# Edge groups' values by DMA copies, two images projected later, first maxima from two queues

## What is computed

```python
y = _layernorm(x)                         # then padded to 28 x 28, cut into 14 x 14 windows
qkv = win.reshape(Nw, 196, C) @ qkv_w + qkv_b
q, k, v = ...                             # 12 heads of 16 channels
attn = q @ k^T * scale + bias_h(q) + bias_w(q)   # relative positions, products of q
attn = softmax(attn)
o = attn @ v
x = shortcut + o @ proj_w + proj_b
x = x + fc2(gelu(fc1(_layernorm(x))))
```

## Time and profile before

| | us |
|---|---|
| median of 3 runs | 362.44 |
| the runs | 361.16 to 362.70 |
| the profiled execution, its own time | 361.79 |
| its span, first to last instruction | 359.7 |
| TensorE matmul busy in it | 340.2 (95%) |
| VectorE, ScalarE, GpSimd busy | 199.9, 146.9, 100.6 |
| mean granted TensorE clock | 0.995 |

### The profile page before, as it was taken

How to read it: one execution, slowest core, us unless ns; L and a number is a source line. 1 busy time by engine, 2 the same in 40 slices (tenths; PEclk the granted TensorE clock), 3 DMA queues, 4 the chain that set the end, 5 groups by cost and what they waited for, 6 DMA issues and landing times.

```text
span 359.7 us, 10564 instructions
## 1 busy us (share of the span) xinstructions
PE 340.2 (95%) x4494; PEld 259.9 (72%) x4494; DVE 199.9 (56%) x483; ACT 146.9 (41%) x326; POOL 100.6 (28%) x192
## 2 busy tenths in 40 slices
PE   6899899999988999999989979999998899999996
PEld 3467587889866548977837768878886643999576
DVE  6362668777767600126846466877785750145472
ACT  2188045555545442023119705555545452202330
POOL 3100507985312039200010050898431204000000
PEclk9899999999999999999999999999999999999999
DMA  7971000000012003010021000000000000000002
GB/s 212 386 244 40 3 5 4 3 6 4 3 24 99 22 1 111 0 66 2 0 89 25 9 3 3 5 3 4 5 5 4 0 2 0 0 2 0 2 0 89
DMA packets 9056, 13.34 MB, mean 37 GB/s; under 512 B 3153, under 2 KB 6609, under 8 KB 9010
## 3 DMA queue, kind: packets, MB, share of 16 engines
q1 hardware_dynamic: 9010, 12.67, 10.9%
HBM read 11.24 MB, written 0.79 MB: 33 GB/s over the span
## 4 chain that ended last, share of the span: by engine, by line
PE 88%; DVE 8%; issue 1%; SPq 1%; DMA 1%; ACT 0%; DVEq 0%
PE banks L912 17%; PE banks L884 13%; PE banks L1001 9%; PE banks L1019 9%; PE banks L929 8%; PE banks L843 6%; PE banks L800 4%; PE banks L771 2%; PE banks L760 2%; PE banks L1185 2%; PE banks L1032 2%; PE banks L1079 2%; DVE negmax L1427 2%; PE banks L819 2%; PE banks L1049 1%
## 5 line engine op out<-in xcount | busy, mean ns | idle before, releaser
L1264 ACT ACTIVATE arena<-banks 128x392 f32<-128x392 f32 (+2 forms) x144 | 62.5, 486 | 60.9 <-PE banks L912 60.9
L884 PE MATMUL banks<-attention_arena 32*128 32x196 f32 x384 | 49.1, 353 | 3.1 <-DVE negmax L1427 1.6
L912 PE MATMUL banks<-attention_arena 32*128 32x196 f32 x384 | 47.5, 342 | 3.3 <-ACT arena L1264 2.0
L1430 DVE TENSOR_REDUCE negmax<-banks 128x4 f32<-128x784 f32 x40 | 39.0, 974 | 14.6 <-PE banks L884 14.3
L912 PE MATMUL banks<-attention_arena,keys 32*128 32x196 f32 x384 | 44.3, 323 | 0.0
L884 PE MATMUL banks<-keys,attention_arena 32*128 32x196 f32 x384 | 44.1, 323 | 0.0
L912 PEld LDWEIGHTS banks<-attention_arena 32*128 32x128 f32 x384 | 30.1, 183 | 10.3 <-issue 7.2
L1001 PE MATMUL banks<-yT,fc 128*128 128x512 f32 (+1 forms) x96 | 33.3, 607 | 0.3
L1019 PEld LDWEIGHTS banks<-fc,arena 128*128 128x128 f32 x192 | 31.1, 190 | 1.5 <-ACT arena L1278 1.5
L884 PEld LDWEIGHTS banks<-attention_arena 32*128 32x128 f32 x384 | 28.2, 183 | 5.6 <-DVE negmax L1427 3.3
L912 PEld LDWEIGHTS banks<-attention_arena,keys 32*128 32x128 f32 x384 | 32.1, 184 | 0.0
(11 more groups left out here) (170 smaller groups left out, 641.2 us busy)
## 6 DMA issues: line engine op xcount, KB each, us to landing
fc<-in_fc SPq DMA_DIRECT2D x2, 768.0 KB, 5.5
qkv<-in_qkv SPq DMA_DIRECT2D x2, 576.0 KB, 4.1
fc<-in_fc SPq DMA_DIRECT2D x2, 576.0 KB, 5.5
attention_arena<-negmaxT SPq DMA_DIRECT2D x72, 1.0 KB
rel<-in_rel SPq DMA_DIRECT2D x2, 448.0 KB, 4.7
x_tok<-in_x SPq DMA_DIRECT2D x4, 192.0 KB, 3.1
inverse<-in_inverse SPq DMA_DIRECT2D x1, 768.0 KB
edge_rel<-negmaxT SPq DMA_DIRECT2D x48, 0.5 KB
```

What stands on the lines that cost most here:

```text
L884: ins = mm(o, asking, asked, start=not with_rel, stop=bool(with_rel))
L912: last = mm(m.bank[4 + j][:, cols * tile:cols * (tile + 1)], keys_of(slot, b, j, tile)[with_rel], queries_of(slot, b, j)[with_rel], start= ...
L1264: run(m.probsT[:, n % P_RING, j, 0:cols], m.bank[4 + j][:, 0:cols], ACT.Exp).then_inc(s.probs, 1)
L1430: dve.tensor_reduce(at[:, 4 * part:4 * part + 4].rearrange("k (j a) -> k j a", a=2), m.banks[:, 2 * part:2 * part + 2, 0:2 * MAIN_KEYS].re ...
```

## The change

Four things are done in each of the two attention blocks.

1. The "v_edge" jobs go, with GpSimd's gather `m.yEdge`. The edge groups' values are copied by SP's DMAs out of the images' rows of `m.v`: 5 DMAs per image (four of 6 or 8 single rows, one of 32 rows; a row is 432 floats, 1,728 bytes). Those of images 0 and 1 stand behind the key moves, as soon as ScalarE has taken the image's values out. Those of images 2 and 3 are issued one at a time behind the maxima of groups 1 to 10. `weigh` of an edge group waits for all 20. GpSimd clears, once at the start, the columns that the whole rows bring along.
2. `project` runs the short products of chunks 0 and 1 of the first half right behind `turn_norm` of the second half, ahead of the second half's full products.
3. The values of images 2 and 3 are projected behind the last rel_h job, ahead of `score` 0. They use banks 4 and 5, so `score` 1 waits until ScalarE has taken them out.
4. Group 0's four maxima DMAs are split: two from SP, two from ScalarE's queue.

```diff
+PROJ += [("v", n, 0, "act") for n in range(2)]
 PROJ += [("rel_w", n, 0, "act") ...] + [("rel_h", n, 0, "dve") ...]
+PROJ += [("v", n, 0, "act") for n in range(2, IMAGES)]
...
+            def move_edge_rows(s, b, piece):
+                if piece == 4:
+                    low = EDGE * SIDE
+                    to, of = m.v[low * b:low * (b + 1), TILES + 1], m.v[128 - low:128, 2 * b + 1]
+                else:
+                    tile, col = divmod(piece, EDGE)
+                    rows, at = min(WIN - 8 * tile, 8), EDGE * (WIN * b + 8 * tile) + col
+                    to = m.v[at:at + EDGE * (rows - 1) + 1:EDGE, TILES]
+                    of = m.v[WIN + col:WIN + col + SIDE * (rows - 1) + 1:SIDE, 2 * b + tile]
+                sp.dma_start(to, of).then_inc(s.v_moved, 16)
...
+                for b in range(2):
+                    wait_for(sp, s.proj_in, *taken_out(job("v", b, 0)))
+                    for piece in range(5):
+                        move_edge_rows(s, b, piece)
                 sp.wait_ge(s.edge_inputs, R_EDGES)
                 for n, (slot, b) in enumerate(GROUPS):
                     sp.wait_ge(s.maxT, n + 1)
+                    for block in range(2 if n == 0 else 0, 4):
+                        sp.dma_start(*max_rows_of(n, block)).then_inc(s.max_rows[n % M_RING], 16)
+                    if 1 <= n <= 10:
+                        move_edge_rows(s, 2 + (n - 1) // 5, (n - 1) % 5)
...
-                for short in (False, True):
-                    for j in range(first, last):
+                for short, jobs in ((False, range(CHUNKS)), (True, range(2)), (False, range(CHUNKS, 2 * CHUNKS)), (True, range(2, 2 * CHUNKS))):
+                    if short and 0 in jobs:
+                        turn_norm(s.ln[0], 0, 1)
+                    for j in jobs:
...
-                    elif h >= 2:
+                    elif h == 1:
+                        wait_for(pe, s.proj_in, *taken_out(job("v", IMAGES - 1, 0)))
+                    else:
                         pe.wait_ge(s.max, h - 1)
...
+                if b >= IMAGES:
+                    pe.wait_ge(s.v_moved, 16 * EDGE_ROWS)     # in weigh; EDGE_ROWS = 5 * IMAGES
...
-                project(l, 0, 2 * CHUNKS)
-                project_values(l)
-                project(l, job("v_edge", 0, 0), job("v_edge", 1, 0) + 1)
-                for j in range(job("rel_w", 0, 0), len(PROJ)):
+                project(l)
+                project_values(l, 0)
+                for j in range(job("rel_w", 0, 0), job("rel_h", SIDE // 2 - 1, 0) + 1):
                     relate(l, j)
+                project_values(l, 2)
...
+                act.wait_ge(s.maxT, 1)
+                act.wait_ge(s.edge_inputs, R_EDGES)
+                for block in range(2):
+                    act.dma_start(*max_rows_of(0, block)).then_inc(s.max_rows[0], 16)
```

More of the change, by code:

```diff
@@ L559, in split, with max_rows_of @@
             return ap[..., FULL * b:FULL * (b + 1)], ap[..., LEFT_AT + LEFT * b:LEFT_AT + LEFT * (b + 1)]
+        def max_rows_of(n, block):
+            slot, b = GROUPS[n]
+            lo, src = 32 * block, m.negmaxT[:, n % M_RING, :]
+            if b >= IMAGES:
+                return m.edgeR[MAX_ROW::GROUP, slot, b - IMAGES, lo:lo + 32], src[lo:lo + 4]
+            dst = m.r[MAX_ROW::GROUP, slot, PLACES * b:PLACES * (b + 1)].rearrange("j (a q) -> j a q", a=2)[:, :, lo:lo + 32]
+            src = src[lo:lo + 8]
+            return (dst[:, 0], src[::2]) if block == 3 else (dst, src)
         block = ctx.enter_context(nc.Block())
@@ L646, in _ @@
                 pool.memset(v_part(slot, 1 - VALUE_HALF[slot]), 1.0).then_inc(v_ones_set, 1)
+            pool.memset(m.v[:, 0:TILES, 8 * GROUP:2 * V_STEP], 0.0).then_inc(v_ones_set, 1)
+            pool.memset(m.v[:, 0:TILES, 2 * V_STEP + 4 * GROUP:], 0.0).then_inc(v_ones_set, 1)
             def attention(l, x_ready):
                 s, wl = A[l], w[l]
[L651 to L655, removed]
                 pool.wait_ge(s.proj_in.dve, taken_out(job("rel_h", SIDE // 2 - 1, 0))[1])
@@ L783, in open_bank, with project @@
                 return m.bank[job_bank(j)]
[L785 removed]
+            def project(l):
                 s, wl = A[l], w[l]
[L788 to L789 removed]
+                for short, jobs in ((False, range(CHUNKS)), (True, range(2)), (False, range(CHUNKS, 2 * CHUNKS)), (True, range(2, 2 * CHUNKS))):
+                    if short and 0 in jobs:
+                        turn_norm(s.ln[0], 0, 1)
+                    for j in jobs:
                         kind, g, part, _ = PROJ[j]
@@ L801, in project, with project_values @@
                                      start=not short, stop=short)
[L802 to L807, removed]
                         if short:
                             ins.then_inc(s.proj_in.pe, 1)
-            def project_values(l):
+            def project_values(l, pair):
                 s, wl = A[l], w[l]
-                first = job("v", 0, 0)
-                for j in range(first, first + IMAGES):
+                first = job("v", pair, 0) - pair
+                for j in range(first + pair, first + pair + 2):
                     bank = open_bank(s, j)
@@ L820, in project_values @@
                            start=tile == 0, stop=False, skip_group_check=True)
[L821 to L828, removed]
+                for tile in range(2):
+                    for j in range(first + pair, first + pair + 2):
+                        rows, at = rest_rows(j), 128 * (2 * (j - first) + tile)
+                        ins = mm(m.bank[job_bank(j)][:, CH * tile:CH * (tile + 1)], m.yT[rows, 1 - j % 2, at:at + 128],
+                                 wl["qkv"][rows, 1 - j % 2, 2 * CH:3 * CH], start=False, stop=True, skip_group_check=True)
+                        if tile == 1:
+                            ins.then_inc(s.proj_in.pe, 1)
             def relate(l, j):
```

29 lines of the change are left out of this document (7 added, 22 removed).

## The result

The changed kernel takes **363.36 us** (median of 20 runs, 360.64 to 367.01) against 361.43 for the kernel before (20 runs beside it): a ratio of **1.0047, 95% interval 1.0024 to 1.0070**. Four of the changed kernel's 20 runs lie over 1.5% above its fastest; the ratio leaves them out, the median doesn't. The prediction was 364.1 from a median of 362.44, +1.7 us; measured are +1.9 by the medians and +1.7 by the ratio. The profiled execution of the changed kernel took 362.05 (before: 361.79), with a span of 360.0 (359.7).

What follows compares the result with a forecast made beforehand. TensorE, busy 95% of the span, was taken as the bound. Per block, 0.25 us gained ahead of the loop and 1.1 lost to the last copy give +0.85, twice +1.7: median 362.44 to 364.1 us, range 361.2 to 366.0.

Steps and rivals of the forecast that it cites:

- Part 2: Block's front: two short steps, 0.93 us, move into TensorE's 1.0 us gap; VectorE's row ends 0.82 us earlier, at 24.55.
- seven operations, then six: VectorE's pauseless row ahead of rel_w: seven operations end at 25.37; with the first done earlier, six end at 24.55.
- Parts 1 and 3, front: Ahead of the loop: rel_w 2.2 us earlier, new TensorE idle 1.8, score 1 waits for ScalarE; 0.25 us gained per block.
- Part 4, nothing: At turn 0: bias_scaled ends last, not the maxima copies, so splitting their issue gains and loses nothing.
- Part 1, the last copy: Behind group 10's maxima: the copy lands 2.2 us after issue, stalling weigh of group 8 by 1.1 us per block.
- the key move: Nearest DMA to the last copy: 64 KB inside the chip's memory, 2.3 us at least, 2.5 in the middle; 2.2 taken.
- rival (b): At weigh of group 8: the last copy lands in time or almost, leaving only the gain, 361.2 to 362.4; chance 0.15.
- the upper end of 1.4: Largest stall forecast at weigh of group 8, in us, with the last copy taking 2.5 us to land.
- The sum: Each block 0.25 us earlier at the loop, 1.1 later inside it, +0.85; two blocks +1.7, median 364.1.
- Rival (a), the clock: The new 1.8 us idle ahead of rel_w halves TensorE's clock: one fall 365.8, one in each block 367.5; chance 0.20.
- Rival (c): Ahead of rel_w: VectorE isn't late, rel_w starts at 22.8, both blocks win 2 us more, 360 is left; chance 0.05.

Runs made afterwards that it cites:

- part 3 undone: The changed kernel with the values of images 2 and 3 projected ahead of the position products again; 361.28 us, ratio 0.9989 to before.
- first repetition: The changed kernel measured again, unchanged, on another chip; 362.97 us, ratio 1.0039 to before.
- part 4 undone: The changed kernel with all four copies of group 0's maxima issued by SP, none by ScalarE; 364.48 us, ratio 1.0088 to before.
- the small copy: The changed kernel with each image's 32-row copy first and a 6-row piece last, measured twice; 363.53 and 363.33 us, ratios 1.0061 and 1.0058 to before.
- the third execution: The profiled execution of the changed kernel's third measurement, nothing altered; that measurement gave 363.08 us, ratio 1.0062 to before.
- the two repetitions: The changed kernel measured two more times, nothing altered; 362.97 and 363.08 us, ratios 1.0039 and 1.0062 to before.
- copies early: The changed kernel with copies of images 2 and 3 issued two at a time behind groups 1 to 5's maxima; 361.10 us, ratio 0.9980 to before.

## Why the prediction was right

The forecast held, and so did the steps it was made of. Three sizes were off and partly cancel: the gain at the front, the landing of the last copy, and its collision with a fetch, which the forecast didn't have.

- **Part 2** hides 0.93 us in the gap, and VectorE's row ends 0.82 earlier: 0.84 measured alone. The row that the prediction calls seven operations, then six, is eight before and seven after; its ends were read from the rows, so the sum doesn't change.
- **Parts 1 and 3, front.** L843 (now L856) 2.2 us earlier: 12.14 - 9.97 = 2.17. A new idle of 1.8: 1.91, ended by VectorE's L1412 (now L1428), as named. `score` 1 waits for ScalarE (L1256): shown, 0.20 at 36.83. The gain that reaches the loop was put at 0.25, with ends -0.1 and 0.6; it is 0.44. With before's `yT` (1.88 us later) `score` 0 starts at 35.67 + 1.88 = 37.55 (predicted 37.6), `score` 1 at 36.83 + 1.88 = 38.71 (38.8), the second maximum at 37.92 + 1.88 = 39.80 (39.9 to 40.0). The mis-sized term is the 0.1 us that I allowed for a semaphore on either side of ScalarE; the chain has 0.04.
- **Part 4, nothing.** `turn` 0 is released by L1485, the former L1469. Right by the trace; the times of the kernel without it (+1.4 us, intervals overlapping) leave a gain open.
- **Part 1, the last copy.** Forecast were a landing of 2.2 us and a stall of 1.1 per block. Shown is a landing of 1.89 to 1.94 and a stall of 1.0 where nothing collides, so the key move was a good neighbour. What the forecast lacked is the collision; rival (b) even took the copy to have nothing else in flight. With an instruction fetch beside it the landing took 3.1 to 3.7 (3.74 with part 3 undone) and the stall became 2.2 to 2.9. That is above the upper end of 1.4. It stood in the first block of four of seven profiled executions with the copies late (after, its first repetition, part 3 undone, part 4 undone; the long one of the small copy isn't counted), and in no second block. In how many timed runs it happens, no run here shows.
- **The sum.** +0.85 per block became, by the traces, +0.5 to +0.6 in a block without the collision and +1.8 to +2.0 in one with it; +1.7 in all became +1.1 (the third execution: 1.01 + 1.08 - 0.44 - 0.51) to +2.5 (the first repetition: 2.42 + 1.08 - 0.44 - 0.51). The medians say +1.9, +1.0 and +1.4, the ratios +1.7, +1.4 and +2.2. That the size came out so near is partly luck: without the collision, the gain at the front and the shorter landing would have left +1.1.
- **Rival (a), the clock.** The idle of 1.91 us ahead of the position products brought no fall, in either block of any profiled execution that had it:

```profile
21.80:25.20 3.40, 2.41 (x60) 2.28 (x64) 0.85 (x2) 1.54 (x4) 0.00 (x0) 1.00 0.55 194
...
193.00:196.00 3.00, 2.21 (x56) 2.11 (x60) 0.64 (x1) 1.24 (x2) 0.00 (x0) 1.00 0.25 42
```

  These are the stretches of the changed kernel around the first position products, clock 1.00 in both. Over the timed runs of the two repetitions the mean granted clock was 0.9958, and 0.9962 for before beside both: a fall more in about one run of eleven, if a fall takes 0.0047. And the loss is there without a fall: at a mean clock of 0.999 or 1.000 the eight runs of the repetitions have a median of 362.1 us, the 22 of before beside them 360.2. Falls in mid-program came elsewhere, behind the longest stall of the last copy (2.87) and, in other kernels, behind idles of 1.01.
- **Rival (b)** fell: no copy landed within 1.1 us. **Rival (c)** fell: VectorE's row has no pause after either.

What the prediction didn't ask is what the front could have given. It found the new idle of 1.8 us and left it as a fact. The values that part 3 moves away were work that would have filled it: moving them won 0.37 us at the position products (10.34 to 9.97) and cost 1.36 at `turn` 0 (28.42 to 29.78). That is 2.7 us in two blocks, more than the whole loss, and the times agree: with the copies early in both, 361.10 us with part 3 and 358.40 without.

## What to carry to other kernels

Work that is moved out from ahead of a wait does not come free when the wait is set by another engine: see first whether the engine would have idled there, and leave it as filler if so. A transfer that hangs on a loop should be issued some loop steps before its reader, not just in time: its landing has a part that hardly depends on its size (1.8 to 1.9 us here at 10 and at 54 KB) and a tail beside an instruction fetch (3.1 to 3.7), which the small copy met too. Measure a block's parts from one event inside the block, such as the scaling of `yT` here: they repeat within 0.1 us, where medians of whole runs leave 1 us open.

## What the runs showed of the hardware

- An instruction fetch of 16 KB (0.88 to 1.17 us) delays the share of a copy that one DMA engine carries. Copies of 54 KB in sixteen shares that met one landed 3.1 to 3.7 us behind their issue instead of 1.9, in four executions; a copy of 10.1 KB in six shares met it once (3.29), and once landed in 1.84 with a fetch beside it.
- Copies inside the chip's memory of 10.1 KB and 54 KB land 1.83 to 1.84 and 1.89 to 1.94 us behind their issue, against 2.3 at the least for a key move of 64 KB.
- In mid-program the granted clock fell to 0.50 behind an idle of TensorE of 2.87 us, and in three other executions behind one of 1.01; it stayed at 1.00 behind idles of 1.91, 2.23, 2.42 and 2.46 and behind 25 others of 1.01. Behind another idle of 2.42 it fell, in the long execution of the small copy. So the length of an idle alone doesn't tell whether the clock falls. A fall of 3.4 us cost 1.3 to 1.7 us.
